# Staggering the per-head RMS scale and moving the final multiply to GpSimd in the q/k stage of a hybrid attention and mixture-of-experts layer

## The chip, the cores and the metric

The program runs on the 8 cores of one Trainium2 chip, each core on one of the 8 batch elements (2048 tokens by 1024 channels) with no traffic between the cores. The metric is the device time in microseconds of the slowest core for one execution.

## What is computed

The layer is four residual blocks in a row, each on a layer-normalized input: a linear attention, a gated mixture of 8 dense experts, a causal differential attention with rotary embedding, and the mixture of experts again. The change is in the third. The part of the reference that it touches:

```python
q = (x @ Wq.T).reshape(B, T, 2, nh // 2, hd)     # 16 groups of hd = 64 in a row of 1024
k = (x @ Wk.T).reshape(B, T, 2, nh // 2, hd)
v = (x @ Wv.T).reshape(B, T, nh // 2, 2 * hd)
q, k = (_rms_norm(q), _rms_norm(k))              # x * rsqrt(mean(x*x over hd) + eps)
q, k = (_apply_rotary(q, cos, sin), _apply_rotary(k, cos, sin))
# [x1*c + x2*s, -x1*s + x2*c] on the two halves of hd
y1 = _causal_attn(q1, k1, v, scale)              # scale = 1/8
y2 = _causal_attn(q2, k2, v, scale)
y = (y1 - lambda_full * y2).reshape(B, T, D)
return y @ Wproj.T
```

## The kernel before

The program is written as five lists of operations, one for each engine, with named semaphore waits; nothing reorders them, so each engine does its operations in the order in which the Python code appends them. A class `_Chained` (L204 to L233) wraps VectorE, ScalarE and GpSimd: each instruction waits until the one before it on the same engine has completed, and the operation's own semaphore is raised in a separate instruction after its last one. All instructions of these three engines are recorded at L205 (L207 in the changed kernel), the DMAs of GpSimd at L199 (L201). The four blocks are separated by barriers over all engines.

The block `phase_attn_b` goes through these stages, one after another: layer norm to DRAM and back transposed (`snt`); projection to v (L989); projection to k with normalization and rotation (`qk_pipeline("k", ...)`); the same for q; reload of q and k transposed from DRAM (L1106, L1113); attention over 8 heads by 2 maps (L1132 scores, L1168 weighted values); the output projection.

`qk_pipeline` (L1007 to L1100) loops over 16 tiles `lc` of 128 tokens, with buffers `b = lc % 2`. One tile is:

- TensorE: 16 matmuls 128x512 (L1016) into two of four PSUM banks; a bank is waited for when its copy of two tiles before is outstanding.
- VectorE, `kev`: two copies of 512 columns each from PSUM into `qr[b]`. Each waits for the rotation of tile `lc - 2`.
- SyncE: load of the cosine and sine rows of the tile into `cs[b]` (L1038), after the rotation of `lc - 2`.
- ScalarE, `rmsq`: square of `qr[b]` into the single buffer `sq`.
- VectorE, `rmsg`: sum of `sq` in 16 groups into `grp`.
- ScalarE, `rmsr`: Ln and Exp, 16 columns each, giving the reciprocal root in `rstdg`.
- For q alone, VectorE: `rstdg` times 0.125.
- GpSimd, `rotary`: six tensor_tensor operations of 512 columns, `qr[b]` and `cs[b]` into the single buffer `rot`. It waits for `rstdg` although it does not read it.
- VectorE, `rscale`: `rot` times `rstdg` spread over the 64 columns of each group, 1024 columns, out in bf16 into `qsb`. It waits for the rotation.
- GpSimd: DMA of `qsb` to `kspill` or `qspill` (L199).

On VectorE the copies of tile `lc + 1` stand behind `rscale` of tile `lc`, since the list is in the order of the loop. After the k stage GpSimd issues the cast of Wq to bf16 in DRAM; SyncE loads it transposed (L972) and the q stage starts.

Of the kernel before, what the change touches and what calls it, by code (L numbers as in the profile page):

```python
# [41 lines left out]
class MK:  # L42
# [26 lines left out]
    def build(self):  # L69
        T, NLC, LT, NLT = self.T, self.NLC, self.LT, self.NLT  # L70
        nc = bass.Bass("TRN2", target_bir_lowering=False)
# [43 lines left out]
        self.epst = nc.alloc_sbuf_tensor("epst", [128, 2], F32)  # L115

        self.P = [nc.alloc_psum_tensor(f"P{i}", [128, 1024], F32) for i in range(4)]

# [1 line left out]

        def init_eps(e):
            e.memset(self.epst[:, 0:1], LN_EPS)
            return e.memset(self.epst[:, 1:2], RMS_EPS)
        self.op("vector", init_eps, inc=("dve", ("init",), 1))
        self._pending_first_wait = {"scalar": [("dve", ("init",))]}

# [748 lines left out]
    def phase_attn_b(self, src, dst):  # L875
        T, NLC, LT, NLT = self.T, self.NLC, self.LT, self.NLT
        ph = f"B{self.nbar}"
        nc, dt, P = self.nc, self.dt, self.P
# [17 lines left out]
        qsb = carve(2 * 1024)  # L896
# [22 lines left out]
        y1 = carvef(NLC * 128)  # L919
        grp = carvef(16)  # L920
        rstdg = carvef(16)
        rz = carvef(2)
        xc2 = [carvef(D), carvef(D)]
        xnew = [carvef(D), carvef(D)]
# [59 lines left out]
        for i in range(nvt):  # L984
# [8 lines left out]
            w = []  # L993
# [12 lines left out]

        def qk_pipeline(which, spillname, scale_q):  # L1007
            wkey = "wk" if which == "k" else "wq"
            for lc in range(NLC):
                b = lc % 2  # L1010
                for it in range(2):
                    i = lc * 2 + it
                    def mmk(e, lc=lc, it=it, i=i):
                        ps = bank4(i)
                        for dk in range(NDK):
                            inst = e.matmul(ps, xnt[:, dk * T + lc * 128: dk * T + lc * 128 + 128],  # L1016
                                            wWb[:, dk * 1024 + it * 512: dk * 1024 + it * 512 + 512],
                                            start=(dk == 0), stop=(dk == NDK - 1))
# [11 lines left out]
                    def kev(e, lc=lc, it=it, i=i, b=b):  # L1030
                        return e.tensor_copy(qr[b][:, it * 512:it * 512 + 512], bank4(i))
                    wkev = [("pe", (ph, which, "mm", i))]
                    if lc >= 2:
                        wkev.append(("pool", (ph, which, "rot", lc - 2)))
                    elif which == "q" and NLC - 2 + lc >= 0:
                        wkev.append(("pool", (ph, "k", "rot", NLC - 2 + lc)))
                    self.op("vector", kev, waits=wkev, inc=("dve", (ph, which, "ev", i), 1))
                self.op("sync", lambda e, lc=lc, b=b: e.dma_start(  # L1038
                    out=cs[b][:], in_=dt["cs_tab"][lc * 128:(lc + 1) * 128, :]),
# [1 line left out]
                          ([("pool", (ph, "k", "rot", NLC - 2)), ("pool", (ph, "k", "rot", NLC - 1))] if which == "q" and NLC >= 2 else []),  # L1041
                    inc=(f"cs{b}", (ph, which, "cs", lc), 16))
                def rmsq(e, b=b):
                    return e.activation(sq[:], qr[b][:], AF.Square)
                self.op("scalar", rmsq, waits=[("dve", (ph, which, "ev", lc * 2 + 1))],
                        inc=("act", (ph, which, "sq", lc), 1))
                def rmsg(e):
                    return e.reduce_sum(grp[:], sq.rearrange("p (g c) -> p g c", g=16), axis=AX.X)
                self.op("vector", rmsg, waits=[("act", (ph, which, "sq", lc))],
                        inc=("dve", (ph, which, "grp", lc), 1))  # L1050
                def rmsr(e, scale_q=scale_q):
                    e.activation(rstdg[:], grp[:], AF.Ln, bias=self.epst[:, 1:2], scale=1.0 / HD)
                    return e.activation(rstdg[:], rstdg[:], AF.Exp, scale=-0.5)
                self.op("scalar", rmsr, waits=[("dve", (ph, which, "grp", lc))],
                        inc=("act", (ph, which, "rstd", lc), 1))
                if scale_q:
                    self.op("vector", lambda e: e.tensor_scalar(
                        rstdg[:], rstdg[:], 0.125, None, ALU.mult),
                        waits=[("act", (ph, which, "rstd", lc))],
                        inc=("dve", (ph, which, "rstds", lc), 1))  # L1060
                    rstd_wait = ("dve", (ph, which, "rstds", lc))
                else:
                    rstd_wait = ("act", (ph, which, "rstd", lc))
                def rotary(e, b=b):
                    q3 = qr[b].rearrange("p (g d) -> p g d", g=16)
                    r3 = rot.rearrange("p (g d) -> p g d", g=16)
# [259 lines left out]
```

How the kernel before makes its waits and increments, by code:

```python
                    def g(*a, **k):  # L196
                        if self._h[0]:
                            self._e.wait_ge(self._sem, self._h[0])
                        return f(*a, **k)
# [2 lines left out]
                    def g(*a, **k):  # L202
                        if self._h[0]:
                            self._e.wait_ge(self._sem, self._h[0])
                        inst = f(*a, **k)
                        inst.then_inc(self._sem, 1)
                        self._h[0] += 1
                        return inst
# [8 lines left out]
                def body(eng, ops=ops, chained=chained, e=e):  # L217
                    holder = [0]
                    proxy = _Chained(eng, self.sems["C" + e], holder) if chained else eng
                    for o in ops:
                        for w in o.waits:
                            s, v = resolve(w)
                            eng.wait_ge(self.sems[s], v)
                        h0 = holder[0]
                        inst = o.fn(proxy) if o.fn is not None else None
                        if o.inc is not None:
                            s, key, n = o.inc
                            if chained and inst is not None and holder[0] > h0:
                                eng.wait_ge(self.sems["C" + e], holder[0])
                                eng.sem_inc(self.sems[s], n)
                            else:
                                if inst is None:
                                    inst = eng.nop()
                                inst.then_inc(self.sems[s], n)
```

## Time and profile before

| | us |
|---|---|
| median of the three timed runs | 11705.65 |
| lowest and highest of them | 11232.61, 11752.51 |
| the profiled execution's own time | 11221.55 |
| its span on the slowest core | 11220.0 |
| spans of the eight cores | 11194.6 to 11220.0 |

The profile is of one execution. Its span runs from the first to the last instruction of a core; 1.55 us of the execution's time lie outside it. Stages are read by their time from the start of the span. The k stage lies at about 5190 to 5480 us, the q stage at 5480 to 5764, both on core 0.

### The profile page before, as it was taken

The numbers are of one execution on the slowest core, as the hardware profiler recorded it, in microseconds if no ns is written. First come the engines' busy times: TensorE is split into PE (matmuls) and PEld (weight loads), VectorE is DVE, ScalarE is ACT, GpSimd is POOL, SyncE is SP. The second block draws the span as 40 slices with busy tenths as digits, with TensorE's granted clock in tenths as the row PEclk, the third lists the DMA queues.
The fourth block names the chain that finished last, engine by engine and source line by source line (L and its number), as shares of the span: only waits on it lengthen the run. The fifth ranks groups of instructions, "written<-read, shape, count | busy, mean of one in ns | idle before, by whom it ended". The sixth has DMA issues, their size and how long they took to land.

```text
span 11220.0 us, 131787 instructions; the slowest of 8 cores (11194.6 to 11220.0 us)
## 1 busy us (share of the span) xinstructions
PE 9018.8 (80%) x39746; PEld 3685.1 (33%) x39746; DVE 4211.8 (38%) x6467; ACT 1633.3 (15%) x2632; POOL 606.4 (5%) x696
## 2 busy tenths in 40 slices
PE   4718999999999999953225553699999999999998
PEld 1303433433333433411112221233333334343333
DVE  1243344344344344351223323244434434434435
ACT  2111111111111111111013331111111111111110
POOL 0000000000000000002420000000000000000000
PEclk9859999999999999976655556799999999999999
DMA  4133222222212222223220005312221222222221
GB/s 89 34 96 51 33 34 40 31 33 31 44 29 39 36 34 37 33 78 70 57 55 5 6 5 136 62 29 34 40 34 29 37 37 31 41 32 34 40 34 40
DMA packets 447064, 474.48 MB, mean 42 GB/s; under 512 B 166936, under 2 KB 364312, under 8 KB 446120
## 3 DMA queue, kind: packets, MB, share of 16 engines
q0 software_dynamic: 271968, 357.66, 19.1%
q1 hardware_dynamic: 174408, 108.39, 4.3%
q8 instruction: 340, 5.57, 0.2%
q14 instruction: 348, 2.85, 0.1%
HBM read 656.91 MB, written 72.35 MB: 65 GB/s over the span
## 4 chain that ended last, share of the span: by engine, by line
PE 72%; DVE 9%; issue 6%; ACT 5%; DMA 3%; POOL 2%; SPq 2%; DVEq 1%; ACTq 1%; POOLq 0%
PE P L849 23%; PE P L766 22%; PE P L770 22%; DVE pf L205 6%; ACT pbf L205 3%; POOL pf L205 2%; PE P L1168 2%; DVE pbf L205 2%; SPq L289 1%; DVE stat L205 1%; ACT pf L205 1%; DMA pf<-xspill 1%; PE P L379 1%; PE P L496 1%; PE P L989 1%
## 5 line engine op out<-in xcount | busy, mean ns | idle before, releaser
L849 PE MATMUL P<-pbf 128*128 128x512 bf16 x11264 | 2888.2, 380 | 368.0 <-DVEq L230 241.2
L205 DVE SCALAR_TENSOR_TENSOR pf<-P,pf 128x512 f32<-128x512 f32 (+1 forms) x3104 | 2345.8, 756 | 1161.4 <-PE P L849 777.8
L766 PE MATMUL P<-pbf 128*128 128x512 bf16 x11264 | 2663.9, 379 | 142.6 <-DMA pbf<-W 142.5
L770 PE MATMUL P<-pbf 128*128 128x512 bf16 x11264 | 2660.9, 379 | 0.0
L205 DVE SCALAR_TENSOR_TENSOR pbf<-P,b_sb,pf 128x512 bf16<-128x512 f32 x1408 | 1056.6, 750 | 3743.6 <-ACTq L230 3743.6
L205 ACT ACTIVATE pf<-P,b_sb 128x512 f32<-128x512 f32 x1408 | 967.3, 687 | 6991.4 <-PE P L770 6991.4
L849 PEld LDWEIGHTS P<-pbf 128*128 128x128 bf16 x11264 | 915.9, 96 | 2325.0 <-issue 1622.7
L766 PEld LDWEIGHTS P<-pbf 128*128 128x128 bf16 x11264 | 1102.2, 98 | 1473.9 <-issue 150.2
L770 PEld LDWEIGHTS P<-pbf 128*128 128x128 bf16 x11264 | 1102.2, 98 | 1329.5 <-issue 0.8
L199 POOL DMA_DIRECT2D pbf<-W x288 | 241.1, 847 | 7720.0 <-PE P L849 7565.4
L205 ACT ACTIVATE pbf<-P 128x512 bf16<-128x512 f32 x800 | 477.7, 597 | 1067.5 <-PE P L1132 494.5
L1132 PE MATMUL P<-pbf 64*128 64x512 bf16 x640 | 336.0, 544 | 283.2 <-ACTq L230 189.4
L1016 PE MATMUL P<-pbf 128*128 128x512 bf16 x512 | 172.8, 514 | 366.1 <-DVEq L230 274.3
L1168 PE MATMUL P<-pbf 128*128 128x129 bf16 x2176 | 228.5, 296 | 232.1 <-DVEq L230 232.1
L205 DVE TENSOR_TENSOR pbf<-pbf 128x512 bf16<-128x512 bf16 x256 | 108.8, 425 | 508.3 <-ACTq L230 487.9
L1168 PEld LDWEIGHTS P<-pbf 128*128 128x128 bf16 x2176 | 210.7, 138 | 263.8 <-issue 260.5
L205 POOL TENSOR_TENSOR pf<-pf 128x512 f32<-128x512 f32 x192 | 240.1, 1250 | 378.4 <-ACTq L230 229.0
L205 ACT ACTIVATE pf<-pf 128x1024 f32<-128x1024 f32 (+1 forms) x146 | 125.7, 861 | 901.5 <-DVEq L230 704.7
L1132 PEld LDWEIGHTS P<-pbf 64*128 64x128 bf16 x640 | 58.8, 100 | 542.6 <-issue 540.9
L656 PE MATMUL P<-pbf 128*128 128x8 bf16 x256 | 11.1, 168 | 269.0 <-DMA pbf<-nspill 263.8
L205 DVE COPY pf<-P 128x512 f32<-128x512 f32 (+1 forms) x88 | 48.0, 546 | 470.3 <-PE P L1016 191.4
L1016 PEld LDWEIGHTS P<-pbf 128*128 128x128 bf16 x512 | 61.9, 125 | 476.9 <-issue 456.6
(81 smaller groups left out, 1617.7 us busy)
## 6 DMA issues: line engine op xcount, KB each, us to landing
pbf<-W POOLq DMA_DIRECT2D x240, 1024.0 KB, 16.5
pf<-xspill SPq DMA_DIRECT2D x64, 512.0 KB, 4.5
xspill<-pf POOLq DMA_DIRECT2D x48, 512.0 KB, 4.8
pbf<-W POOLq DMA_DIRECT2D x48, 512.0 KB, 12.0
pf<-x SPq DMA_DIRECT2D x32, 512.0 KB, 4.5
nspill<-pbf POOLq DMA_DIRECT2D x64, 256.0 KB, 4.2
pf<-cs_tab SPq DMA_DIRECT2D x32, 512.0 KB, 3.6
y<-pf POOLq DMA_DIRECT2D x16, 512.0 KB, 2.9
```

What stands on the lines that cost most here:

```text
L199: return f(*a, **k)
L205: inst = f(*a, **k)
L289: self.op("sync", lambda e, dk=dk: e.dma_start(out=xnt[:, dk * T:(dk + 1) * T], in_=self.dt["nspill"][:, dk * 128:(dk + 1) * 128], transpo ...
L379: inst = e.matmul(ps[:], xnt[:, dk * T + lc * 128: dk * T + lc * 128 + 128], wW[:, dk * 1024 + et * 512: dk * 1024 + et * 512 + 512], star ...
L496: inst = e.matmul(ps[:, :LT], ctx_sb[:, dk * 1024 + evk * 128: dk * 1024 + evk * 128 + 128], eq_sb[:, dk * T + lt * LT: dk * T + lt * LT + ...
L766: e.matmul(pa, w1v[:, dk * cw + hk * 128: dk * cw + hk * 128 + 128], xnt[:, dk * T + lt * LT: dk * T + lt * LT + LT], start=(dk == 0), sto ...
L770: inst = e.matmul(pb_, w2v[:, dk * cw + hk * 128: dk * cw + hk * 128 + 128], xnt[:, dk * T + lt * LT: dk * T + lt * LT + LT], start=(dk == ...
L849: inst = e.matmul(ps, hb[:, hk * T + lc * 128: hk * T + lc * 128 + 128], w3v[:, hk * 1024 + dtile * 512: hk * 1024 + dtile * 512 + 512], s ...
L989: inst = e.matmul(ps, xnt[:, dk * T + lc * 128: dk * T + lc * 128 + 128], wWb[:, dk * 1024 + it * 512: dk * 1024 + it * 512 + 512], start= ...
L1016: inst = e.matmul(ps, xnt[:, dk * T + lc * 128: dk * T + lc * 128 + 128], wWb[:, dk * 1024 + it * 512: dk * 1024 + it * 512 + 512], start= ...
L1132: return e.matmul(ps_s, kT[off:off + HD, ik * T + kt * 128: ik * T + kt * 128 + 128], qT[off:off + HD, ik * T + qt * QT: ik * T + qt * QT ...
L1168: inst = e.matmul(ps_y, E_sb[:, kt * 512 + qc * 128: kt * 512 + qc * 128 + 128], vx[:, kt * 1032 + h * VDE: kt * 1032 + h * VDE + VDE], st ...
```

## The change

It does the following, all but the constants in `qk_pipeline`:

- `rscale` goes from VectorE's list to GpSimd's, between the rotation and the DMA of the same tile.
- The rotation no longer waits for `rstdg`; `rscale` does.
- Ln and Exp of a tile are written in ScalarE's list behind the square of the next tile (`pend_rstd`, `emit_rstd`), the last ones behind the loop.
- `sq` of this stage, `grp` and `rstdg` get a buffer for each parity (`sqb`, 16 columns each of `grp` and `rstdg`), with waits for the use of two tiles before.
- The factor 0.125 of q goes into the Exp as a bias of ln 0.125, read from a column of `epst`; the VectorE operation goes. k reads a column of zeros.
- Of the two copies only the first waits for the rotation of two tiles before.

```diff
@@ init @@
-            return e.memset(self.epst[:, 1:2], RMS_EPS)
+            e.memset(self.epst[:, 1:2], RMS_EPS)
+            e.memset(self.epst[:, 2:3], float(np.log(0.125)))
+            return e.memset(self.epst[:, 3:4], 0.0)
@@ qk_pipeline @@
+            pend_rstd = []
+
+            def emit_rstd(lc):
+                b = lc % 2
+                def rmsr(e, b=b, lc=lc):
+                    e.activation(rstdg[:, b * 16:b * 16 + 16], grp[:, b * 16:b * 16 + 16],
+                                 AF.Ln, bias=self.epst[:, 1:2], scale=1.0 / HD)
+                    bias2 = self.epst[:, 2:3] if scale_q else self.epst[:, 3:4]
+                    return e.activation(rstdg[:, b * 16:b * 16 + 16],
+                                        rstdg[:, b * 16:b * 16 + 16],
+                                        AF.Exp, scale=-0.5, bias=bias2)
+                w = [("dve", (ph, which, "grp", lc))]
+                if lc >= 2:
+                    w.append(("pool", (ph, which, "qsb", lc - 2)))
+                self.op("scalar", rmsr, waits=w, inc=("act", (ph, which, "rstd", lc), 1))
...
-                    if lc >= 2:
-                        wkev.append(("pool", (ph, which, "rot", lc - 2)))
+                    if it == 0:
+                        if lc >= 2:
+                            wkev.append(("pool", (ph, which, "rot", lc - 2)))
...
-                    return e.activation(sq[:], qr[b][:], AF.Square)
-                self.op("scalar", rmsq, waits=[("dve", (ph, which, "ev", lc * 2 + 1))],
-                        inc=("act", (ph, which, "sq", lc), 1))
+                    return e.activation(sqb[:, b * 1024:(b + 1) * 1024], qr[b][:], AF.Square)
+                wsq = [("dve", (ph, which, "ev", lc * 2 + 1))]
+                if lc >= 2:
+                    wsq.append(("dve", (ph, which, "grp", lc - 2)))
+                self.op("scalar", rmsq, waits=wsq, inc=("act", (ph, which, "sq", lc), 1))
...
-                self.op("scalar", rmsr, waits=[("dve", (ph, which, "grp", lc))],
-                        inc=("act", (ph, which, "rstd", lc), 1))
-                if scale_q:
-                    self.op("vector", lambda e: e.tensor_scalar(
-                        rstdg[:], rstdg[:], 0.125, None, ALU.mult),
-                        waits=[("act", (ph, which, "rstd", lc))],
-                        inc=("dve", (ph, which, "rstds", lc), 1))
...
+                pend_rstd.append(lc)
+                if len(pend_rstd) > 1:
+                    emit_rstd(pend_rstd.pop(0))
...
                 self.op("gpsimd", rotary,
-                        waits=[(f"cs{b}", (ph, which, "cs", lc)), rstd_wait,
+                        waits=[(f"cs{b}", (ph, which, "cs", lc)),
                                ("dve", (ph, which, "ev", lc * 2 + 1))],
...
-                    rb = rstdg[:].unsqueeze(2).broadcast_to([128, 16, HD])
+                    rb = rstdg[:, b * 16:b * 16 + 16].unsqueeze(2).broadcast_to([128, 16, HD])
                     return e.tensor_tensor(o3, r3, rb, ALU.mult)
-                wrs = [("pool", (ph, which, "rot", lc))]
+                wrs = [("act", (ph, which, "rstd", lc))]
...
-                self.op("vector", rscale, waits=wrs, inc=("dve", (ph, which, "qsb", lc), 1))
+                self.op("gpsimd", rscale, waits=wrs, inc=("pool", (ph, which, "qsb", lc), 1))
...
+            while pend_rstd:
+                emit_rstd(pend_rstd.pop(0))
```

How the instructions stand, first GpSimd at the first tiles of the k stage, before and after (`pf` is the pool of fp32 tiles, `pbf` that of bf16 tiles; the six `pf<-pf` of a tile are its rotation):

```order
L205 TENSOR_TENSOR pf<-pf 128x16x32
L205 TENSOR_TENSOR pf<-pf 128x512
L205 TENSOR_TENSOR pf<-pf 128x16x32 x2
L205 TENSOR_TENSOR pf<-pf 128x512
L205 TENSOR_TENSOR pf<-pf 128x16x32
L199 DMA kspill<-pbf 128x1024
L205 TENSOR_TENSOR pf<-pf 128x16x32
```

```order
L207 TENSOR_TENSOR pf<-pf 128x16x32
L207 TENSOR_TENSOR pf<-pf 128x512
L207 TENSOR_TENSOR pf<-pf 128x16x32 x2
L207 TENSOR_TENSOR pf<-pf 128x512
L207 TENSOR_TENSOR pf<-pf 128x16x32
L207 TENSOR_TENSOR pbf<-pf 128x1024
L201 DMA kspill<-pbf 128x1024
L207 TENSOR_TENSOR pf<-pf 128x16x32
```

A seventh tensor_tensor, of 1024 columns, now stands between a tile's rotation and its DMA. On VectorE at the same tiles, before and after (COPY x2 are the two copies, TENSOR_REDUCE the group sums):

```order
L205 COPY pf<-P 128x512 x2
L205 TENSOR_REDUCE pf<-pf 128x16
L205 TENSOR_TENSOR pbf<-pf 128x1024
L205 COPY pf<-P 128x512 x2
L205 TENSOR_REDUCE pf<-pf 128x16
L205 TENSOR_TENSOR pbf<-pf 128x1024
```

```order
L207 COPY pf<-P 128x512 x2
L207 TENSOR_REDUCE pf<-pf 128x16
L207 COPY pf<-P 128x512 x2
L207 TENSOR_REDUCE pf<-pf 128x16
L207 COPY pf<-P 128x512 x2
```

The multiply that stood between the group sums of one tile and the copies of the next is gone from there. On ScalarE at the same tiles, before and after (128x1024 is the square, the 128x16 rows are Ln and Exp):

```order
L205 ACTIVATE pf<-pf 128x1024
L205 ACTIVATE pf<-pf,epst 128x16
L205 ACTIVATE pf<-pf 128x16
L205 ACTIVATE pf<-pf 128x1024
L205 ACTIVATE pf<-pf,epst 128x16
L205 ACTIVATE pf<-pf 128x16
```

```order
L207 ACTIVATE pf<-pf 128x1024 x2
L207 ACTIVATE pf<-pf,epst 128x16 x2
L207 ACTIVATE pf<-pf 128x1024
L207 ACTIVATE pf<-pf,epst 128x16 x2
L207 ACTIVATE pf<-pf 128x1024
```

Ln and Exp of the first tile now stand behind the square of the second, and so on, one tile late.

## Rows read from the trace of the kernel before

**Rows 1.** The page: span, then TensorE's busy time, share and instructions.
```profile
span 11220.0 us, 131787 instructions; the slowest of 8 cores (11194.6 to 11220.0 us)
PE 9018.8 (80%) x39746; PEld 3685.1 (33%) x39746; DVE 4211.8 (38%) x6467; ACT 1633.3 (15%) x2632; POOL 606.4 (5%) x696
```

**Rows 2.** Windows: k stage, q stage, attention; us, busy by engine, clock, DMA, GB/s.
```profile
5190.00:5480.00 290.00, 87.11 (x256) 31.05 (x256) 61.29 (x65) 25.27 (x48) 130.01 (x113) 0.64 0.21 55
5480.00:5764.00 284.00, 85.65 (x256) 30.90 (x256) 64.03 (x80) 25.27 (x48) 128.82 (x111) 0.65 0.18 51
5830.00:6770.00 940.00, 534.87 (x2687) 257.24 (x2688) 286.15 (x976) 365.62 (x613) 8.12 (x7) 0.58 0.02 5
```

**Rows 3.** Timeline, one tile of the k stage (start, duration, work, idle before, releaser).
```profile
5312.51 1.23 DVE L205 TENSOR_TENSOR pbf<-pf 128x1024 bf16<-128x1024 f32 x1 [10.10 <-POOLq L230]
5314.14 0.69 DVE L205 COPY pf<-P 128x512 f32<-128x512 f32 x1 [0.40 <-DVE pbf L205]
5314.46 0.59 POOL L199 DMA_DIRECT2D kspill<-pbf  x1 [2.29 <-DVEq L230]
...
5315.08 6.26 PE L1016 MATMUL P<-pbf 128*128 128x512 bf16 x16 [10.41 <-DVEq L230]
5315.23 0.69 DVE L205 COPY pf<-P 128x512 f32<-128x512 f32 x1 [0.40 <-DVE pf L205]
...
5316.18 1.06 ACT L205 ACTIVATE pf<-pf 128x1024 f32<-128x1024 f32 x1 [12.89 <-DVEq L230]
...
5317.49 1.22 DVE L205 TENSOR_REDUCE pf<-pf 128x16 f32<-128x1024 f32 x1 [1.57 <-ACTq L230]
...
5318.96 0.31 ACT L205 ACTIVATE pf<-pf,epst 128x16 f32<-128x16 f32 x1 [1.73 <-DVEq L230]
...
5319.36 0.22 ACT L205 ACTIVATE pf<-pf 128x16 f32<-128x16 f32 x1
...
5319.94 8.23 POOL L205 TENSOR_TENSOR pf<-pf 128x512 f32<-128x512 f32 x6 [4.89 <-ACTq L230]
...
5328.50 1.23 DVE L205 TENSOR_TENSOR pbf<-pf 128x1024 bf16<-128x1024 f32 x1 [9.80 <-POOLq L230]
```

**Rows 4.** Timeline of GpSimd: first and last tile of k, first and last of q.
```profile
5207.63 8.23 POOL L205 TENSOR_TENSOR pf<-pf 128x512 f32<-128x512 f32 x6 [154.55 <-ACTq L230]
5218.10 0.62 POOL L199 DMA_DIRECT2D kspill<-pbf  x1 [2.24 <-DVEq L230]
...
5459.60 0.59 POOL L199 DMA_DIRECT2D kspill<-pbf  x1 [2.29 <-DVEq L230]
5460.18 0.52 POOL L199 DMA_DIRECT2D bWqs<-bWq  x1
5504.99 8.23 POOL L205 TENSOR_TENSOR pf<-pf 128x512 f32<-128x512 f32 x6 [44.29 <-DVEq L230]
5515.52 0.60 POOL L199 DMA_DIRECT2D qspill<-pbf  x1 [2.30 <-DVEq L230]
...
5764.28 0.59 POOL L199 DMA_DIRECT2D qspill<-pbf  x1 [2.28 <-DVEq L230]
```

**Rows 5.** The chain of waits behind the last tile of q.
```profile
5764.28 2.33 DMA qspill<-pbf
```

**Rows 6.** Groups by form over both stages: GpSimd, VectorE.
```profile
L205 POOL TENSOR_TENSOR pf<-pf 128x512 f32<-128x512 f32 x192 | 240.1, 1250 | 378.4 <-ACTq L230 229.0 <-DVEq L230 125.8 <-POOL pf L205 0.9
...
L205 DVE COPY pf<-P 128x512 f32<-128x512 f32 x64 | 44.2, 691 | 216.7 <-PE P L1016 191.4 <-DVE pf L205 13.0 <-DVE pbf L205 12.3
L205 DVE TENSOR_TENSOR pbf<-pf 128x1024 bf16<-128x1024 f32 x32 | 39.2, 1225 | 301.2 <-POOLq L230 301.2
L205 DVE TENSOR_REDUCE pf<-pf 128x16 f32<-128x1024 f32 x32 | 39.0, 1219 | 50.5 <-ACTq L230 50.5
L205 DVE TENSOR_SCALAR pf<-pf 128x16 f32<-128x16 f32 x16 | 2.8, 174 | 18.7 <-ACTq L230 18.7
```

**Rows 7.** DMA issues: the cosine and sine loads, KB each, median us to landing.
```profile
pf<-cs_tab SPq DMA_DIRECT2D x32, 512.0 KB, 3.6
```

More of the change, by code:

```diff
@@ L114, in build @@
         self.lam_col = nc.alloc_sbuf_tensor("lam_col", [128, 1], F32)
-        self.epst = nc.alloc_sbuf_tensor("epst", [128, 2], F32)
+        self.epst = nc.alloc_sbuf_tensor("epst", [128, 4], F32)
         self.P = [nc.alloc_psum_tensor(f"P{i}", [128, 1024], F32) for i in range(4)]
@@ L919, in phase_attn_b @@
         y1 = carvef(NLC * 128)
-        grp = carvef(16)
-        rstdg = carvef(16)
+        sqb = carvef(2 * D)
+        grp = carvef(32)
+        rstdg = carvef(32)
         rz = carvef(2)
@@ L1029, in qk_pipeline, with kev @@
                     self.op("tensor", mmk, waits=w, inc=("pe", (ph, which, "mm", i), 1))
-                    def kev(e, lc=lc, it=it, i=i, b=b):
+                    def kev(e, it=it, i=i, b=b):
                         return e.tensor_copy(qr[b][:, it * 512:it * 512 + 512], bank4(i))
                     wkev = [("pe", (ph, which, "mm", i))]
-                    if lc >= 2:
-                        wkev.append(("pool", (ph, which, "rot", lc - 2)))
-                    elif which == "q" and NLC - 2 + lc >= 0:
-                        wkev.append(("pool", (ph, "k", "rot", NLC - 2 + lc)))
+                    if it == 0:
+                        if lc >= 2:
+                            wkev.append(("pool", (ph, which, "rot", lc - 2)))
+                        elif which == "q" and NLC - 2 + lc >= 0:
+                            wkev.append(("pool", (ph, "k", "rot", NLC - 2 + lc)))
                     self.op("vector", kev, waits=wkev, inc=("dve", (ph, which, "ev", i), 1))
@@ L1043, in rmsq, with rmsg @@
                 def rmsq(e, b=b):
-                    return e.activation(sq[:], qr[b][:], AF.Square)
-                self.op("scalar", rmsq, waits=[("dve", (ph, which, "ev", lc * 2 + 1))],
-                        inc=("act", (ph, which, "sq", lc), 1))
-                def rmsg(e):
-                    return e.reduce_sum(grp[:], sq.rearrange("p (g c) -> p g c", g=16), axis=AX.X)
+                    return e.activation(sqb[:, b * 1024:(b + 1) * 1024], qr[b][:], AF.Square)
[3 more added lines that the diff above has]
+                self.op("scalar", rmsq, waits=wsq, inc=("act", (ph, which, "sq", lc), 1))
+                def rmsg(e, b=b):
+                    return e.reduce_sum(grp[:, b * 16:b * 16 + 16],
+                                        sqb[:, b * 1024:(b + 1) * 1024]
+                                        .rearrange("p (g c) -> p g c", g=16), axis=AX.X)
                 self.op("vector", rmsg, waits=[("act", (ph, which, "sq", lc))],
                         inc=("dve", (ph, which, "grp", lc), 1))
-                def rmsr(e, scale_q=scale_q):
-                    e.activation(rstdg[:], grp[:], AF.Ln, bias=self.epst[:, 1:2], scale=1.0 / HD)
-                    return e.activation(rstdg[:], rstdg[:], AF.Exp, scale=-0.5)
-                self.op("scalar", rmsr, waits=[("dve", (ph, which, "grp", lc))],
-                        inc=("act", (ph, which, "rstd", lc), 1))
-                if scale_q:
-                    self.op("vector", lambda e: e.tensor_scalar(
-                        rstdg[:], rstdg[:], 0.125, None, ALU.mult),
-                        waits=[("act", (ph, which, "rstd", lc))],
-                        inc=("dve", (ph, which, "rstds", lc), 1))
-                    rstd_wait = ("dve", (ph, which, "rstds", lc))
-                else:
-                    rstd_wait = ("act", (ph, which, "rstd", lc))
+                pend_rstd.append(lc)
+                if len(pend_rstd) > 1:
+                    emit_rstd(pend_rstd.pop(0))
                 def rotary(e, b=b):
@@ L1095, in qk_pipeline @@
                     in_=qsb[:, b * 1024:(b + 1) * 1024]),
-                    waits=[("dve", (ph, which, "qsb", lc))],
+                    waits=[("pool", (ph, which, "qsb", lc))],
                     inc=(f"sp2{lc % 2}", (ph, which, "sp", lc), 16))
+            while pend_rstd:
+                emit_rstd(pend_rstd.pop(0))
             if which == "k":
```

## The prediction

> **What bounds the kernel now.** I read the page first, for the size of the place. The span is 11220.0 us and TensorE is busy for 80% of it [rows 1]; the change does not touch the stages that make this share. Then the windows by stage. In the k and the q stage, 290 and 284 us, no engine is near full: TensorE 87 and 86 us, VectorE 61 and 64, ScalarE 25 and 25, GpSimd 130 and 129 [rows 2]. Where the busiest engine is at 45%, a ring of waits sets the time, and the timeline of one tile shows the ring [rows 3]. The reader should follow it there: VectorE multiplies (5312.51), copies twice (5314.14, 5315.23), ScalarE squares (5316.18), VectorE sums (5317.49), ScalarE does Ln and Exp (5318.96, 5319.36), GpSimd rotates for 8.23 us (5319.94), and VectorE multiplies again at 5328.50. From multiply to multiply it is 5328.50 - 5312.51 = 15.99 us, and all of it is in series. Two things close the ring: the rotation waits for a factor that it does not read, and the copies of the next tile stand behind a multiply that waits for the rotation. TensorE's 6.26 us for 16 matmuls lie inside and are waited for by nobody here [rows 3].
>
> The mean period is read over a whole stage, from DMA issue to DMA issue on GpSimd. For k: (5459.60 - 5218.10)/15 = 16.10 us. For q: (5764.28 - 5515.52)/15 = 16.58 us [rows 4]. The 0.48 us more of q are the extra VectorE operation, 0.17 us and its two hand-overs [rows 6].
>
> Is the end of each stage on the path of the whole program? Behind the last k tile GpSimd issues the cast of Wq at once (5460.18), and q cannot start without it [rows 4]; behind the last q tile the chain of waits goes through its DMA at 5764.28 [rows 5] into the transposed reloads and the attention. So what the two stages lose in length, the kernel loses in length.
>
> **The change part by part.** *The rotation without the wait for the factor, and the multiply on GpSimd.* VectorE no longer waits for the rotation of the same tile, only for that of two tiles before. The copies of the next tile can run during the rotation, and GpSimd becomes the engine that never waits. Its period is then its own work for a tile:
>
> - six rotations with their gaps, 8.23 us [rows 3];
> - the hand-over to the multiply. Inside the rotation a gap is (8.23 - 6 x 1.25)/5 = 0.15 us [rows 3, 6]; across engines, rotation end (5328.17) to multiply start (5328.50), it is 0.33 us. Between operations of one engine there is a semaphore raised and one more wait, so I take 0.25 us;
> - the multiply of 1024 columns. No GpSimd operation of this form is in the trace. The nearest is its own 512-column operation of 1250 ns [rows 6]; twice the columns is 2.50 us, which I take. Lower bound: VectorE's 1.23 us for the same operation [rows 6]. Upper bound: twice the GpSimd price for a column, 5.00 us, for the bf16 output and the spread operand;
> - hand-over to the DMA 0.25 us, issue 0.59 us [rows 3], hand-over to the next rotation 0.15 us.
>
> Sum: 8.23 + 0.25 + 2.50 + 0.25 + 0.59 + 0.15 = 11.97 us. The DMA issue does not hold up what stands behind it: 5459.60 + 0.59 is where the next one starts [rows 4].
>
> On the price of the multiply, the Trainium skill ("GPSIMD Engine Reference", section 3.1) gives 4497 ns for a GpSimd tensor_tensor of 2048 fp32 columns and calls elementwise work there about twice as dear as on VectorE, a rule that speaks against moving a multiply to it. A line through that figure and the 1250 ns row would give an estimate of 2.33 us here, and the sum would be 5 us better. The row and the rule agree in direction: 1250 ns for 512 columns on one, 1225 ns for 1024 on the other [rows 6].
>
> *Does the factor come in time?* Ln and Exp of tile n now wait for the square of tile n+1, hence for its copies, hence for the rotation of tile n-1. From the end of that rotation: 0.33 hand-over, two copies 2 x 0.69 with 0.40 between, 0.30, square 1.06, Ln and Exp with gaps 0.7: some 4.2 us [rows 3]. The multiply of tile n starts 3.74 us (the tail of tile n-1) plus 8.23 + 0.25 later, at 12.2 us. That leaves 8 us of cover. The group sums of tile n were made earlier; VectorE has 2 x 0.69 + 1.22 = 2.60 us of work in 11.97.
>
> *The cosine load* waits for the rotation of two tiles before and lands in 3.6 us [rows 7], against a whole multiply, DMA and rotation (12 us) until it is read. *TensorE* needs 6.26 us for a tile, below 11.97. *Second buffers* for squares, sums and factors cost nothing and only keep the stagger free of waits. *The factor 0.125 in the Exp* removes 0.48 us for each q tile, already inside the 16.58. *Two more memsets* at the start, and a bias operand on 32 Exps of 0.22 us, lie beside other work: below 1 us if not.
>
> *Ends of the stages.* The first rotation no longer waits for square, sum, Ln and Exp: copies end at 5315.92, the rotation starts at 5319.94, 4.02 us, of which 0.3 stay: 3.7 us less for k, 4.2 for q. The last tile pays 0.25 + 2.50 + 0.25 = 3.00 us between rotation and DMA, against 2.26 now [rows 4]: 0.75 more for each stage.
>
> Total: k 15 x (16.10 - 11.97) = 62.0, q 15 x (16.58 - 11.97) = 69.2, ends (3.7 - 0.75) + (4.2 - 0.75) = 6.4, together 137.5 us (the load of Wq between the stages and the reloads behind q are unchanged). In general, with a multiply of T us, the gain is 217.5 - 32 T.
>
> **Which time it is taken from.** The profiled execution took 11221.55 us itself. It is 11 us under the lowest of the three timed runs and 484 under their median, 11705.65. Forecast: 11221.55 - 137.5 = 11084 us. By the bounds of T: 1.23 us gives a gain of 178, 11043 us; 5.00 us gives 57.5, 11164 us.
>
> **The rivals.**
>
> *A. GpSimd and VectorE hinder each other.* Today no VectorE instruction of these stages runs during a rotation, so the trace does not show whether they can [rows 3]. After the change all 2.60 us of VectorE work of a tile fall under GpSimd work. If each of its instructions stopped GpSimd for its whole length, the period would be 11.97 + 2.60 = 14.57, and the gain 15 x 1.53 + 15 x 2.01 + 6.4 = 59.5 us: 11162 us. For it: the overlap is new. Against it: the copies read PSUM and only the sums read SBUF. On this the Trainium skill ("SBUF — State Buffer", section "Who interferes with whom") says that GpSimd shares a port pair with VectorE, that a VectorE instruction with two SBUF inputs or in a two-port mode blocks it, and that one with a single SBUF input outside these modes does not. By that rule rival A is empty, since the two-input multiply is just what leaves VectorE. No row here shows it.
>
> *B. The multiply is slow on GpSimd (slower than before).* The place is the one new instruction, 32 times. The gain is nothing at T = 217.5/32 = 6.8 us and negative beyond. With three times the price for a column, 7.5 us, because the output is narrowed to bf16 and one operand is spread with a step of zero, the kernel loses 22.5 us: 11244 us. A loss of 2% needs T = 13.8 us. For it: none of GpSimd's 192 tensor_tensor rows has either trait. Against it: the halves of 32 columns, in 16 groups, cost the same 1250 ns as the plain forms [rows 6], and VectorE does the same operation, with both traits, in 1225 ns [rows 6].
>
> *C. The factor comes late.* If the staggered Ln and Exp reached the multiply last, the ring would be closed through ScalarE. It has 8 us of cover; to cost anything the hand-overs would have to treble. If the ring stayed whole as now, the period would be that of today less the extra q operation: a gain of 15 x 0.48 = 7 us, 11214 us.
>
> *D. TensorE's clock in the attention behind it.* There the granted clock is 0.58 and TensorE busy 534.87 of 940 us, waiting and working by turns [rows 2]. If the shorter stages ahead left it at 0.9, its work would shrink to 345 us and up to 190 us more would go: 10894 us. Against it: the attention's own waits are unchanged, and it holds the low level for 940 us, not just at its start.
>
> **How the numbers follow.** Forecast with T between its bounds 0.76; A 0.09; B 0.06; C 0.03; D 0.06. About 2% (224 us) is what a measurement of this kernel can tell from no change. Faster by more than that needs D: 0.06. Slower by more needs B with T over 13.8: 0.04 of its 0.06. Within 2%: 0.90.
>
> The likeliest case has 11043 to 11164 us as its own range, and A lies inside it. But the three runs shown lie 520 us apart, and a median of such runs after the change may stand where the one before does: 11705.65 - 137.5 = 11568, and from the highest run 11752.51 - 137.5 = 11615. I give that a chance of over 2 in 10, so the range goes from 11040 to 11620; it takes in B and C as well.
>
> **What would show it.** Right: DMA issues on GpSimd some 12.0 us apart in both stages, k and q alike; GpSimd's idle before the rotation gone from 4.9 to about 0.15 us; the multiply near 2.5 us in GpSimd's groups; VectorE's copies and sums lying under the rotation; later stages of the old length. The step on the multiply is wrong if its row stands far from 2.5 us. A is right if the rotation rows grow over 1250 ns or VectorE's over 691 and 1219 ns. C is right if the multiply is released by ScalarE. D is right if the granted clock of the attention is no longer 0.58. The whole is wrong if the two stages shrink by a good deal less or more than 68 us each, or if they shrink and the rest grows by as much.

## The result and the profile after

The ratio of the changed kernel to the kernel before is 0.9873, with a 95% interval from 0.985 to 0.9895: 1.3% faster, which is less than the 2% that the prediction took as the least clear change. The lowest time is 11082.14 us against 11224.76 before, 142.6 us less. In many executions of either kernel the cores of one die or of both show a lower granted clock and take longer, so the medians, 11563.01 us of 8 executions and 11716.14 of 10, mix two levels and do not compare well. The traces below are read on core 4, where the granted clock was the same 0.90 to 0.91 in both, and rows of before are of core 4 too where a number is not in the rows shown ahead of the prediction.

The timeline of GpSimd in the k stage after the change answers to [rows 4] (start, duration, work, idle before with its releaser):

```profile
5205.91 0.61 POOL L201 DMA_DIRECT2D kspill<-pbf  x1 [0.78 <-POOLq L232]
5206.54 8.25 POOL L207 TENSOR_TENSOR pf<-pf 128x512 f32<-128x512 f32 x6
5215.14 1.90 POOL L207 TENSOR_TENSOR pbf<-pf 128x1024 bf16<-128x1024 f32 x1 [0.34 <-POOL pf L207]
...
5385.34 0.59 POOL L201 DMA_DIRECT2D kspill<-pbf  x1 [0.76 <-POOLq L232]
5385.92 0.52 POOL L201 DMA_DIRECT2D bWqs<-bWq  x1
5433.58 0.60 POOL L201 DMA_DIRECT2D qspill<-pbf  x1 [0.77 <-POOLq L232]
...
5612.99 0.59 POOL L201 DMA_DIRECT2D qspill<-pbf  x1 [0.76 <-POOLq L232]
```

The reader is to see that the rotation has no idle time before it: GpSimd goes from DMA to rotation to multiply to DMA and waits only for its own completions. The mean period is (5385.34 - 5205.91)/15 = 11.96 us for k and (5612.99 - 5433.58)/15 = 11.96 us for q, where it was 16.10 and 16.59 on this core.

The timeline of all engines over one tile answers to [rows 3]:

```profile
5238.88 0.69 DVE L207 COPY pf<-P 128x512 f32<-128x512 f32 x1 [7.02 <-POOLq L232]
5239.02 1.90 POOL L207 TENSOR_TENSOR pbf<-pf 128x1024 bf16<-128x1024 f32 x1 [0.40 <-POOL pf L207]
5239.83 5.01 PE L1035 MATMUL P<-pbf 128*128 128x512 bf16 x16 [5.90 <-DVEq L232]
5239.91 0.69 DVE L207 COPY pf<-P 128x512 f32<-128x512 f32 x1 [0.33 <-DVE pf L207]
5240.91 1.06 ACT L207 ACTIVATE pf<-pf 128x1024 f32<-128x1024 f32 x1 [9.21 <-DVEq L232]
5241.68 0.59 POOL L201 DMA_DIRECT2D kspill<-pbf  x1 [0.76 <-POOLq L232]
5242.22 1.22 DVE L207 TENSOR_REDUCE pf<-pf 128x16 f32<-128x1024 f32 x1 [1.62 <-ACTq L232]
5242.29 0.71 ACT L207 ACTIVATE pf<-pf,epst 128x16 f32<-128x16 f32 x2 [0.32 <-ACT pf L207]
5242.29 8.26 POOL L207 TENSOR_TENSOR pf<-pf 128x512 f32<-128x512 f32 x6
5250.81 0.69 DVE L207 COPY pf<-P 128x512 f32<-128x512 f32 x1 [7.38 <-POOLq L232]
5250.95 1.90 POOL L207 TENSOR_TENSOR pbf<-pf 128x1024 bf16<-128x1024 f32 x1 [0.40 <-POOL pf L207]
```

Everything but GpSimd now waits: VectorE sits idle for 7 us before its copies, ScalarE for 9 us before its square, TensorE for 6 us. The factor is ready at 5243.00 (5242.29 + 0.71), 8 us before the multiply that reads it, at 5250.95.

The groups over both stages, answering to [rows 6]:

```profile
L207 POOL TENSOR_TENSOR pf<-pf 128x512 f32<-128x512 f32 x192 | 241.2, 1256 | 211.2 <-DVEq L232 187.1 <-POOL pf L207 0.9
L207 POOL TENSOR_TENSOR pbf<-pf 128x1024 bf16<-128x1024 f32 x32 | 60.8, 1901 | 12.8 <-POOL pf L207 12.8
...
L207 DVE COPY pf<-P 128x512 f32<-128x512 f32 x64 | 44.3, 692 | 414.2 <-PE P L1035 209.1 <-POOLq L232 194.5 <-DVE pf L207 10.7
L207 DVE TENSOR_REDUCE pf<-pf 128x16 f32<-128x1024 f32 x32 | 39.0, 1220 | 52.0 <-ACTq L232 52.0
```

The rotation's idle time is 211.2 us, of which all but some 24 us are the two waits for the first tile of a stage (187.1 us). Its operations take 1256 ns where they took 1250, VectorE's 692 and 1220 where they took 691 and 1219, although they now run at the same time. The attention behind is unchanged. The windows of 940 us in it, before and after, both on core 4, answer to [rows 2]:

```profile
5830.00:6770.00 940.00, 537.61 (x2696) 258.58 (x2695) 286.63 (x980) 366.44 (x614) 8.11 (x7) 0.58 0.02 5
5690.00:6630.00 940.00, 535.97 (x2695) 258.12 (x2695) 286.61 (x980) 365.88 (x613) 8.12 (x7) 0.58 0.02 5
```

TensorE's busy time (537.61 and 535.97 us) and the granted clock (0.58) are where they were.

### The profile page after: what moved, and what is told of

The parts are those of the page before. It is cut to its first block, busy times and chain, and to the rows that moved or that the text cites. A ratio compares the mean times of both kernels' runs of the same rounds, so it can differ in the third digit from the quotient of the medians.

```text
span 11600.1 us, 131705 instructions; the slowest of 8 cores (11055.5 to 11600.1 us)
## 1 busy us (share of the span) xinstructions
PE 9630.9 (83%) x39746; PEld 3888.3 (34%) x39746; DVE 4170.1 (36%) x6421; ACT 1636.2 (14%) x2632; POOL 668.2 (6%) x728
## 4 chain that ended last, share of the span: by engine, by line
PE 74%; DVE 7%; issue 5%; ACT 4%; DMA 3%; POOL 3%; SPq 2%; DVEq 1%; ACTq 0%; POOLq 0%
PE P L768 23%; PE P L772 23%; PE P L851 23%; DVE pf L207 5%; ACT pbf L207 3%; POOL pf L207 2%; PE P L1184 2%; DVE pbf L207 2%; SPq L291 1%; DVE stat L207 1%; PE P L381 1%; PE P L498 1%; PE P L402 1%; PE P L992 1%; PE P L438 1%
## 5 line engine op out<-in xcount | busy, mean ns | idle before, releaser
L851 PE MATMUL P<-pbf 128*128 128x512 bf16 x11264 | 2975.0, 403 | 287.2 <-DVEq L232 207.5
L768 PE MATMUL P<-pbf 128*128 128x512 bf16 x11264 | 2894.8, 404 | 140.7 <-DMA pbf<-W 140.7
L772 PE MATMUL P<-pbf 128*128 128x512 bf16 x11264 | 2889.5, 403 | 0.0
L851 PEld LDWEIGHTS P<-pbf 128*128 128x128 bf16 x11264 | 996.5, 100 | 2249.1 <-issue 1820.7
L768 PEld LDWEIGHTS P<-pbf 128*128 128x128 bf16 x11264 | 1154.9, 103 | 1644.2 <-issue 880.4
L772 PEld LDWEIGHTS P<-pbf 128*128 128x128 bf16 x11264 | 1154.2, 102 | 1500.1 <-issue 731.0
L1035 PE MATMUL P<-pbf 128*128 128x512 bf16 x512 | 177.6, 526 | 225.5 <-DVEq L232 131.6
L1184 PEld LDWEIGHTS P<-pbf 128*128 128x128 bf16 x2176 | 210.9, 138 | 263.3 <-issue 260.0
L207 POOL TENSOR_TENSOR pf<-pf 128x512 f32<-128x512 f32 x192 | 241.2, 1256 | 224.9 <-DVEq L232 200.8
L992 PE MATMUL P<-pbf 128*128 128x512 bf16 x256 | 68.6, 442 | 149.7 <-DMA pbf<-bWvs 149.7
```

What stands on the lines that cost most here:

```text
L207: inst = f(*a, **k)
L768: e.matmul(pa, w1v[:, dk * cw + hk * 128: dk * cw + hk * 128 + 128], xnt[:, dk * T + lt * LT: dk * T + lt * LT + LT], start=(dk == 0), sto ...
L772: inst = e.matmul(pb_, w2v[:, dk * cw + hk * 128: dk * cw + hk * 128 + 128], xnt[:, dk * T + lt * LT: dk * T + lt * LT + LT], start=(dk == ...
L851: inst = e.matmul(ps, hb[:, hk * T + lc * 128: hk * T + lc * 128 + 128], w3v[:, hk * 1024 + dtile * 512: hk * 1024 + dtile * 512 + 512], s ...
L1184: inst = e.matmul(ps_y, E_sb[:, kt * 512 + qc * 128: kt * 512 + qc * 128 + 128], vx[:, kt * 1032 + h * VDE: kt * 1032 + h * VDE + VDE], st ...
```

## The experiments

For each kernel the period was read as above, from DMA issue to DMA issue or, where the DMA moved, from rotation to rotation, on core 4 where no other core is named. Each of e1, e2, e3, e7, e9 and e10 was executed one to three times, so for them the period in the trace is the result and a time is only its companion.

**e1: only the wait is moved.** The kernel before, with the multiply on VectorE:

```diff
-                        waits=[(f"cs{b}", (ph, which, "cs", lc)), rstd_wait,
+                        waits=[(f"cs{b}", (ph, which, "cs", lc)),
...
-                wrs = [("pool", (ph, which, "rot", lc))]
+                wrs = [("pool", (ph, which, "rot", lc)), rstd_wait]
```

> The kernel before with one wait moved: the rotation no longer waits for the factor, the multiply on VectorE does. My theory: of the 16.1 us ring only square, sum, Ln and Exp leave it (4 us), so the period becomes rotation 8.23 + hand-over 0.33 + multiply 1.23 + copies 2 x 0.69 with gaps 0.80 + hand-over 0.3 = 12.3 us in k and in q, nearly all of the whole change's gain. Rival: the multiply's place on VectorE is what matters (the copies behind it), and the period stays above 14 us until it is moved.

Measured: 12.45 us in k and 12.47 in q, span of core 4 11081.3 us. One tile, in the timeline:

```profile
5251.35 8.26 POOL L205 TENSOR_TENSOR pf<-pf 128x512 f32<-128x512 f32 x6 [1.19 <-DVEq L230]
...
5260.01 1.23 DVE L205 TENSOR_TENSOR pbf<-pf 128x1024 bf16<-128x1024 f32 x1 [6.20 <-POOLq L230]
5261.64 0.69 DVE L205 COPY pf<-P 128x512 f32<-128x512 f32 x1 [0.40 <-DVE pbf L205]
5261.97 0.59 POOL L199 DMA_DIRECT2D kspill<-pbf  x1 [2.36 <-DVEq L230]
...
5262.73 0.69 DVE L205 COPY pf<-P 128x512 f32<-128x512 f32 x1 [0.40 <-DVE pf L205]
...
5263.75 8.26 POOL L205 TENSOR_TENSOR pf<-pf 128x512 f32<-128x512 f32 x6 [1.19 <-DVEq L230]
```

The ring is still closed through VectorE, as rotation, multiply, copy, copy, rotation. But square, sum, Ln and Exp (4 us) are out of it, and so is the extra VectorE operation of q, since q's period is now that of k. Of the 4.14 us that a k tile loses in the full change, 16.10 - 12.45 = 3.65 us come from two lines about one wait.

**e2: the multiply is moved, the wait stays.** The changed kernel, without the stagger and with the rotation waiting for the factor again. The second buffers, the single wait of the copies and the bias in the Exp are still in it; no run takes these out.

```diff
-                if len(pend_rstd) > 1:
+                if pend_rstd:
...
                         waits=[(f"cs{b}", (ph, which, "cs", lc)),
+                               ("act", (ph, which, "rstd", lc)),
```

> The changed kernel with the multiply on GpSimd, but the rotation waits for the factor as before and Ln and Exp are not staggered. My theory: with the multiply gone from VectorE the factor is ready during the rotation before, so the wait is free and the period is 11.96 us as in the full change. Rival: the wait still costs its 4 us and the period is 14 to 16 us.

Measured: 11.98 and 12.00 us, lowest time 11080.66 us, the full change's within 2 us. One tile, in the timeline:

```profile
5257.91 0.59 POOL L201 DMA_DIRECT2D kspill<-pbf  x1 [0.76 <-POOLq L232]
5258.44 1.22 DVE L207 TENSOR_REDUCE pf<-pf 128x16 f32<-128x1024 f32 x1 [1.62 <-ACTq L232]
5258.52 8.26 POOL L207 TENSOR_TENSOR pf<-pf 128x512 f32<-128x512 f32 x6
...
5259.97 0.71 ACT L207 ACTIVATE pf<-pf,epst 128x16 f32<-128x16 f32 x2 [1.79 <-DVEq L232]
```

The rotation starts right behind the DMA issue, with no idle time. With the multiply gone from VectorE, copies, square, sum, Ln and Exp of a tile are done before the rotation of the tile before it ends (here at 5260.68, 6 us before that end), and the wait for the factor is free. So either cut alone opens most of the ring.

**e3: only the stagger is undone** (the first of e2's two edits).

> The changed kernel with Ln and Exp right behind the square and sum of their own tile. My theory: the stagger is worth nothing, period 11.96 us in k and q, VectorE and ScalarE still wait for the rotation. Rival: without the stagger ScalarE holds up the multiply and the period grows by 0.5 us or more.

Measured: 11.96 and 11.96 us, lowest time 11076.03 us. The stagger of Ln and Exp is worth nothing in the period.

**e7: the multiply twice on GpSimd.**

```diff
+                    e.tensor_tensor(o3, r3, rb, ALU.mult)
                     return e.tensor_tensor(o3, r3, rb, ALU.mult)
```

> The changed kernel with the multiply done twice on GpSimd (the second writes the same values again). My theory, GpSimd never waits and its own work is the period: 11.96 + 1.90 + 0.14 = 14.0 us in both stages, 32 x 2.04 = 65 us more in all. Rival: something else sets 11.96 us (VectorE's copies, the loads) and the period grows by less than 1 us.

Measured: 14.01 us in both stages, 11145.02 us, 62.9 us over the changed kernel's lowest time. That is 2.05 us more for each tile, the multiply's 1.90 and a gap of 0.15, so GpSimd's own work is the period. The gain falls with the multiply's length as the prediction's 32 T has it, with the gap added.

**e4: the multiply on VectorE, one tile late.** `rscale` of tile `lc - 1` goes to VectorE's list behind the sums of tile `lc`, with two rotation buffers; GpSimd issues the DMA of `lc - 1` behind the rotation of `lc`.

```diff
-        rot = carvef(D)
+        rot2 = [carvef(D), carvef(D)]
...
+                if lc >= 1:
+                    emit_scale(lc - 1)          # VectorE
                 def rotary(e, b=b):
...
+                if lc >= 1:
+                    emit_spill(lc - 1)          # DMA, GpSimd
```

> The multiply is back on VectorE, but one tile late: it stands behind the copies and sum of the next tile, with two rotation buffers, and GpSimd issues a tile's DMA behind the next rotation. My theory: GpSimd's work is the period, 8.25 + hand-over 0.4 to 0.76 + issue 0.59 = 9.3 to 9.6 us, some 2.4 us x 32 = 77 us less than the changed kernel, so about 11005 us. Rival, VectorE's two-input multiply and GpSimd's rotation now run at the same time and stop each other: the multiply's row grows beyond 1.23 us towards 2.5, or the rotation by up to 1.23 us, and the period is 10.8 us.

Measured: 9.72 us between rotations, just above the 9.3 to 9.6 expected, and a lowest time of 11000.28 us; the ratio to before is 0.9813 (0.9771 to 0.9855). This interval and that of the changed kernel touch, and it is the period, 9.72 against 11.96 us, that sets the two apart. The multiply kept its 1225 ns and the rotation mostly its 8.3 us, which looked like a refutation of the rival. But now and then a rotation took 8.66 us or more, 9.20 in the second k tile, and e5 showed why.

**e5: e4 with the DMA off GpSimd.** The tiles' DMAs are issued by ScalarE, and the cast of Wq before the k stage.

```diff
-                self.op("gpsimd", lambda e, lc=lc, b=b, spillname=spillname: e.dma_start(
+                self.op("scalar", lambda e, lc=lc, b=b, spillname=spillname: e.dma_start(
...
+        wcast("bWq", "wq")
         qk_pipeline("k", "kspill", False)
-        wprep("bWq", wWb, "wq", waits=[("pe", (ph, "k", "mm", NLC * 2 - 1))])
+        wprep("bWq", wWb, "wq", cast=False, waits=[("pe", (ph, "k", "mm", NLC * 2 - 1))])
```

> e4, with the DMAs of the tiles issued by ScalarE (before its square of two tiles later) and the cast of Wq issued before the k stage. My theory: the period falls by the issue and its hand-over to 8.25 + 0.2 to 0.4 = 8.5 to 8.7 us, and the gap between the stages (48 us from cast to the first q DMA) shrinks by some 30 us or more, so 60 us less than e4, about 10945 us. Rival: TensorE at its low clock (6.3 us and a hand-over for a tile) or the square waiting behind the DMA on ScalarE sets the period at 9.5 us or more.

Measured on core 0, granted clock 0.909: 9.67 us between rotations in k and 9.69 in q, not 8.6, and a span of 10973.1 us against 10992.3 on the same core in e4. That is 19 us less where 60 were expected. GpSimd's idle time between the stages did fall, from 38.1 us in e4 to 8.4. But the earlier cast of Wq took most of it back ahead of the k stage, where SyncE loads the layer norm's output transposed, e4 and then e5, both on core 0:

```profile
5047.68 52.94 SPq L291 DMA_TRANSPOSE pbf<-nspill  x8
```

```profile
5045.62 72.74 SPq L291 DMA_TRANSPOSE pbf<-nspill  x8
```

With a third weight cast of 2048 KB issued just before them, these loads take 20 us longer, and GpSimd's idle time ahead of the first k rotation grows from 148.1 to 167.2 us. Of the 30 us won between the stages some 10 are left.

The period hardly fell. Two timeline rows of e4 (core 4) and three of e5 (the last of them a window that ends in the first rotation operation) show what took its place:

```profile
5266.79 1.23 DVE L207 TENSOR_TENSOR pbf<-pf 128x1024 bf16<-128x1024 f32 x1 [3.88 <-POOLq L232]
5266.85 0.59 POOL L201 DMA_DIRECT2D kspill<-pbf  x1 [0.76 <-POOL pf L207]
```

```profile
5259.03 1.23 DVE L207 TENSOR_TENSOR pbf<-pf 128x1024 bf16<-128x1024 f32 x1 [3.52 <-POOLq L232]
5259.16 9.21 POOL L207 TENSOR_TENSOR pf<-pf 128x512 f32<-128x512 f32 x6 [0.47 <-POOL pf L207]
...
5259.16 2.21 POOL L207 TENSOR_TENSOR pf<-pf 128x512 f32<-128x512 f32 x1 [0.47 <-POOL pf L207]
```

In e4 the multiply mostly lay beside the DMA issue, with 0.2 us left over into a rotation of 8.33 us. In the tile shown it reaches 0.57 us into the rotation, which takes 8.68 us. In e5 it lies 1.10 us deep in a rotation of 9.21 us, whose first operation takes 2.21 us instead of 1.25: the rotation grows with the overlap. What the DMA issue gave up, this longer operation took. That the multiply is what holds it up is still a reading of rows here; e9 and e10 put it to the test.

**e9 and e10: what stops what.** The changed kernel with one more VectorE operation for each tile, under the rotation, its result unused, both with the same waits. In e9 it reads two SBUF tiles, in e10 one:

```diff
+                    e.tensor_tensor(xnew[0][:], sqb[:, b * 1024:(b + 1) * 1024], cs[b][:], ALU.mult)
```

```diff
+                    e.reduce_sum(xnew[0][:, 0:16], sqb[:, b * 1024:(b + 1) * 1024]
+                                 .rearrange("p (g c) -> p g c", g=16), axis=AX.X)
```

> The changed kernel with one more VectorE operation for each tile ahead of the group sums, a multiply of two fp32 tiles in SBUF (1024 columns, result unused). It falls under GpSimd's rotation. After e4 and e5 my theory is that a VectorE instruction with two SBUF inputs stops a GpSimd instruction: the period grows from 11.96 by about the length of the multiply, to 12.9 to 13.2 us, in one rotation operation of some 2.3 us. Rival: what e5 showed comes from something else (the back-to-back start), and the period stays at 12.0 us, as VectorE has idle time enough.

> As e9 with the same waits, but the added VectorE operation reads one SBUF tile (the group sums made a second time, 1.22 us, result unused). My theory: one input does not stop GpSimd, the period stays at 11.96 to 12.05 us and the rotation at 8.25. Rival: any VectorE work that reads SBUF stops GpSimd, and the period grows as in e9.

Measured, on core 0: 12.73 us in both stages of e9, 11.98 in both of e10. The groups of e9, then those of e10:

```profile
L207 POOL TENSOR_TENSOR pf<-pf 128x512 f32<-128x512 f32 x192 | 266.8, 1390 | 209.0 <-DVEq L232 184.8 <-POOL pf L207 0.9
...
L207 DVE TENSOR_TENSOR pf<-pf 128x1024 f32<-128x1024 f32 x32 | 62.2, 1945 | 64.3 <-DMA pf<-cs_tab 54.0 <-ACTq L232 10.3
```

```profile
L207 POOL TENSOR_TENSOR pf<-pf 128x512 f32<-128x512 f32 x192 | 241.8, 1259 | 209.0 <-DVEq L232 184.8 <-POOL pf L207 0.9
...
L207 DVE TENSOR_REDUCE pf<-pf 128x16 f32<-128x1024 f32 x64 | 78.1, 1220 | 66.8 <-DMA pf<-cs_tab 53.2 <-ACTq L232 10.3
```

With one input both engines keep their times. With two, both lose: the rotation's operations go from 1256 to 1390 ns in the mean, and the multiply takes up to 2.48 us where the shortest took 1.23. One tile of e9 shows them taking turns. The first row is VectorE's, of the timeline; the others are the tile's first three GpSimd operations, of the chain of waits:

```profile
5254.23 2.48 DVE L207 TENSOR_TENSOR pf<-pf 128x1024 f32<-128x1024 f32 x1 [1.86 <-DMA pf<-cs_tab]
```

```profile
5254.35 1.28 POOL pf L207
...
5255.76 2.07 POOL pf L207
...
5257.97 1.26 POOL pf L207
```

VectorE's record ends at 5256.71, 1.1 us after GpSimd's first operation ended at 5255.63; the second starts its record at 5255.76, but ends at 5257.83, 1.1 us after VectorE's. The ends come in turn, each about one undisturbed instruction after the other engine's, which reads as each waiting out a whole instruction of the other. The expectation of 12.9 to 13.2 us was a little high: it had the whole 1.23 us added, and 0.8 was.

**e8: two of the six rotation products on VectorE as well,** on top of e5:

```diff
+                    e.tensor_tensor(t3, q3[:, :, 32:64], s3, ALU.mult)
+                    return e.tensor_tensor(t4, q3[:, :, 0:32], s3, ALU.mult)
+                self.op("vector", prods, waits=[(f"cs{b}", (ph, which, "cs", lc))],
+                        inc=("dve", (ph, which, "pr", lc), 1))
...
-                    e.tensor_tensor(t3, q2, s3, ALU.mult)
...
-                    e.tensor_tensor(t4, q1, s3, ALU.mult)
```

> e5 with two of the six rotation products on VectorE (both factors in SBUF). My theory: GpSimd's own work falls to 4 x 1.25 with gaps = 5.4 us and hand-over 0.47, and it is stopped by VectorE's multiply (0.95) and two products (about 1.2 in all), so the period becomes 8.0 us instead of 9.68, some 30 x 1.65 = 50 us less than e5, about 10925 us. Rival: VectorE becomes the bound, 3.83 + 1.2 us of work and its hand-overs in series with the rotation through the copies, period 9 us or more. A second rival: TensorE at its low clock holds it at 7 us and above.

> e8 once more, for its ratio to the kernel before. Theory: the gain seen in the cores' spans (from about 11205 to 10930) holds as a ratio of times, 0.975 with an interval that ends below 0.985. Rival: the work moved to VectorE costs something outside the two stages and the ratio is no better than e4's 0.981.

Measured: 8.05 us in most tiles, lowest times 10936.07 and 10937.26 us in the two series. Against the lowest times of before beside them (11211.02 and 11234.06) that is 0.975 and 0.974. There is no interval for it: e8's place ahead of e4 rests on these two single times, against three of e4 from 11000.28 to 11001.13, and on the period. On core 0 the span is 40 us below e5's, where 50 were expected. The size was nearly as expected, the bound was not. The timeline rows of a tile on core 0:

```profile
5246.09 0.69 DVE L207 COPY pf<-P 128x512 f32<-128x512 f32 x1 [0.40 <-DVE pbf L207]
...
5247.11 0.69 DVE L207 COPY pf<-P 128x512 f32<-128x512 f32 x1 [0.33 <-DVE pf L207]
...
5248.14 1.49 DVE L207 TENSOR_TENSOR pf<-pf 128x512 f32<-128x512 f32 x2 [0.33 <-DVE pf L207]
...
5249.95 1.22 DVE L207 TENSOR_REDUCE pf<-pf 128x16 f32<-128x1024 f32 x1 [0.33 <-DVE pf L207]
5249.99 6.25 POOL L207 TENSOR_TENSOR pf<-pf 128x512 f32<-128x512 f32 x4 [1.80 <-DVEq L232]
5251.65 2.09 DVE L207 TENSOR_TENSOR pbf<-pf 128x1024 bf16<-128x1024 f32 x1 [0.47 <-DVE pf L207]
```

VectorE now has no wait but its own hand-overs, and GpSimd waits 1.80 us for it. VectorE's multiply takes 2.09 us instead of 1.23 beside a rotation of 6.25 us, where four operations with their gaps need 5.4: the two hold each other up as in e9. The rival "VectorE becomes the bound" is right in kind, at 8.05 and not 9 us.

## Why the prediction was right or wrong

**The number and its level: wrong as it was put.** The forecast was 11084 us beside a median before of 11705.65, which read together say 622 us or 5.3% less; the kernel is 1.3% faster, 142.6 us between the lowest times. The step that failed is "Which time it is taken from": the gain of 137.5 us was subtracted from the profiled execution's own 11221.55 us, 484 us below the median that stood beside it, and only that level's time was given as the forecast. At its own level it was right: the lowest time is 11082.14. At the median's level the text had 11568, and the measured median is 11563.01; that these agree within 5 us is luck, since the kernel before alone had medians of 11552.1, 11746.93 and 11948.21 us in three later series of 7, 7 and 11 executions. A forecast given as a difference or ratio, 137.5 us or 0.988 of the profiled 11221.55, would have said what was meant; the measured ratio is 0.9873.

**The ring: right.** Its two closures were named, and e1 and e2 show each. What the prediction did not say is that either of the two, opened alone, gives nearly the whole gain: 12.45 and 11.98 us in k, of 16.10 before.

**The period: right by a sum whose parts were off.** 11.97 us was forecast, 11.96 measured. The parts by the rows above:

| part of the period | forecast | measured |
|---|---|---|
| six rotations | 8.23 | 8.25 |
| hand-over to the multiply | 0.25 | 0.40 |
| multiply, 1024 columns | 2.50 | 1.90 |
| hand-over to the DMA | 0.25 | 0.76 |
| issue | 0.59 | 0.59 |
| hand-over to the next rotation | 0.15 | 0.02 |

The measured parts add to 11.92; two periods of each stage with one gap longer by 0.24 to 0.29 us (1.00 to 1.04 us instead of 0.76 before the DMA, or 0.43 instead of 0.14 inside a rotation) lift the mean. The multiply was sized 0.6 us too long, by doubling the 512-column row; the two hand-overs 0.66 us too short together. That they cancel is luck. The way from a rotation's end to the DMA issue was a row already: 2.29 us before the DMA held 0.33, the multiply's 1.23, and so 0.73 behind it, which I could have read. The estimate from the Trainium skill ("GPSIMD Engine Reference", section 3.1), 2.33 us, was nearer than the doubled row and still too long. Why 1024 columns cost 1.5 times 512 and not twice was not tried. VectorE's copies beside the multiply are not part of its price: the last tile of k, behind which no copy is left in the stage, has the same 1.90 us (5382.68 on core 4).

**The whole gain: right.** On core 4 k loses 241.5 - 179.4 = 62.1 us (forecast 62.0), q 248.8 - 179.4 = 69.4 (69.2), and the ends and what lies between the stages 7 us (6.4). The last agrees in part by chance: ahead of k's first DMA it is 1.3 us where 2.95 were forecast, between the stages 3.9 where it was 3.45, and behind q 1.9 where the reloads were to be unchanged. Attention starts 140.6 us earlier on the trace's clock, 2.1 us of which the trace already has at the first v matmul.

**The factor's cover: right,** at 8 us. e3 adds what the prediction did not say: the stagger, in the form in which it was made, only spends cover. Without it the factor is ready some 18 us before its multiply, with it 8.

**Rival A** (GpSimd and VectorE hinder each other) did not happen in the changed kernel (1256 ns against 1250), for the reason given: no VectorE instruction with two SBUF inputs is left under GpSimd's work. The rule of the Trainium skill ("SBUF — State Buffer", section "Who interferes with whom") agrees with e9 and e10, 12.73 against 11.98 us, in both directions. **Rival B** did not: 1.90 us against the 6.8 at which the gain is gone. **Rival C** did not: no multiply waits for ScalarE. **Rival D** did not: the granted clock stayed at 0.58.

## What to carry to other kernels

Before dividing work anew, look in a ring of waits for a wait on something that the waiting operation does not read: here the two lines of e1 brought 3.65 of the 4.14 us that a k tile gained. When the ring opens, the period is the busiest engine's own work with its hand-overs, and a hand-over is to be read from the trace for each pair: GpSimd's three in a tile (0.40, 0.76 and 0.02 us) are 1.18 us together, beside a multiply of 1.90. When VectorE and GpSimd are to share a stage, keep VectorE's operations with two SBUF inputs out from under GpSimd's, or beside its DMA issue. Where that can't be done, add their price: a multiply of 1.23 us made the period 0.8 us longer in e9. It can still pay, as e8 shows. A DMA that is moved forward is to be priced where it then lies: two thirds of what e5's earlier cast won between the stages went ahead of them. And a forecast is given as a difference or a ratio, with the level it starts from.

## What the runs showed of the hardware

A VectorE tensor_tensor with both inputs in SBUF and a GpSimd tensor_tensor hold each other up, and by the ends of their records in e9 they take turns by whole instructions: 1.25 us became 2.21 us on GpSimd (e5), 1.23 became 2.48 on VectorE (e9) and 2.09 (e8). The waiting time stands inside the waiting instruction's duration, so it shows as a slow operation and not as idle time before it. VectorE's copies out of PSUM and its sums over one SBUF tile cost GpSimd's operations less than 10 ns (1256 ns in the changed kernel and 1259 in e10, against 1250).

On GpSimd a multiply of 1024 columns with a bf16 output and a spread operand took 1901 ns, 512 columns with fp32 output 1250 ns. Before its own DMA issue GpSimd spent 0.76 us behind its last operation, before its next tensor_tensor inside an operation 0.14 us, and behind the issue 0.02 us.

The eight transposed loads of the layer norm's output took 72.74 us instead of 52.94 when three weight casts of 2048 KB each, from DRAM to DRAM, were issued just before them and not two (e5 and e4, core 0).
